# Mask and maximum in one VectorE instruction, a full-height last down block, and three roots by ScalarE

## The chip, the cores and the metric

The kernel runs on one core of a Trainium2 chip. The metric is the device time of one execution in microseconds (us): 378.05 us is the median of three executions of the kernel before. The core has a matrix engine (TensorE, PE in the profile, its weight loads PEld), an elementwise engine (VectorE, DVE), an activation engine (ScalarE, ACT), a general engine (GpSimd, POOL) and a queue that issues transfers (SyncE, SP). Each works through its own list of instructions in order; they wait for each other by counting semaphores.

## The reference

Two transformer layers on `x` of 4 sequences by 256 rows by 256 columns, that is 1024 tokens:

```
x = x + xattn0(layernorm(x), ctx)      # 16 heads, rope, softmax over 256 keys
x = x + ffn0(layernorm(x))             # fp8 emulation: x8 = (x/s).astype(e4m3), s = max|x|/448
                                       # out = (square(relu(x8 @ Wfc8.T * s*sw)) to fp8) @ Wpr8.T
n = layernorm(x)
s = ((ctx @ Wq.T + bq) @ (ctx @ Wk.T + bk).T) / 8 * n      # scores times the normed x
x = x + softmax(where(mask, -inf, s))
n = layernorm(x)
routed = sigmoid(n @ w_router + b) > 0.5
h  = n + rmsnorm(n) * w1 @ wv @ wo     # plus biases
y  = h + (silu(h2 @ w_gate) * (h2 @ w_up)) @ w_down        # h2 = rmsnorm(h) * w2, 704 hidden
x  = x + where(routed, y, n)
```

## The kernel before

The 1024 tokens are eight tiles of 128 rows (`NT = 8`). All inputs of one stage stay on the chip. Each engine has one block of Python that writes its list in the order in which it runs; nothing is planned by a scheduler, so the order of the lines is the order of the work, and a wait stops everything behind it on that engine. `in_order` on VectorE and GpSimd makes an engine wait for its own last instruction.

The stages, with their times in the trace: the 16-head attention fills about the first 253 us. `project_last` leaves four pairs of tiles in the accumulator banks, and `x1_tiles` on VectorE adds each pair to `xs`, takes statistics, and the largest and smallest value of each row. The last pair is written out below it. Its variances go to GpSimd, whose `power(3, ...)` forms the reciprocal root; `newton(3, rstd)` refines it on VectorE, and the largest normed value goes through TensorE (`turn_largest`, `largest_everywhere`) to all rows, as the fp8 scale. TensorE's products for the query and key rows (line 1805) stand ahead of `turn_largest` and wait until the last pair has been added.

Then come the fp8 rows, `expand`, the squares on ScalarE (`z_square`), and from about 280 us `contract(t)`, which needs the two fp8 parts of tile t: `h8_shared` from VectorE, and `h8_halved` from VectorE followed by `rounded_top` on ScalarE. `x2_tile(t)` adds the result to `xs`.

The second attention works in two halves of four tiles: `gate_scores`, `mask_scores`, `largest` on VectorE, `root` on GpSimd, `softmax` (exponentials) on ScalarE, `x3_sums` and `x3_statistics` on VectorE. From these variances the function `newton(n, ...)` makes three reciprocal roots per half (numbers 5, 6, 7 and 9, 10, 11), each from a first value that GpSimd computes by a power. `normalise` and `norm_rows` write the normed rows, `turn_norm(c)` transposes them on TensorE, `turned_copy` on ScalarE copies them, and `attend(c)` multiplies them with the folded value and output weights into one bank per tile. `h_tile` takes the result; the sum of its squares (`h_square_sum`, ScalarE), `h_square`, the third root and `h2_tiles` lead to the next transposes, `turn(2, atbuf, ...)`. On TensorE, `keep_busy` issues products whose result nobody reads.

The gated network works on 512 tokens at a time, in six blocks of the 704 hidden columns: five of 128 and one of 64. `gate_high` and `gate_low` fill two banks, `silus` reads one, `gated` the other; `high_part` and `low_part` split the product into two parts for precision. `down(t, fts)` adds up the blocks of one tile. In a full block a `product` is three products; in the last block the high and the low part lie above each other in one tile of 128 rows (`gated_hi[0:64]` and `gated_hi[64:128]`), so two are enough, and the second used only the upper 64 rows. `wd`, and with it `wd_rest`, holds the last 64 rows of `w_down` twice, above each other.

ScalarE's functions stand in tables that are loaded by an instruction of its own (`ACT_TABLE_LOAD`); the kernel before has two of them, one at the start and one ahead of the first `Silu`.

Of the kernel before, what the change touches and what calls it, by code (L numbers as in the profile page):

```python
# [23 lines left out]
P = 128  # L24
# [14 lines left out]
FP8_SHARED = 240.0  # L39
MASKED = -1.5e35  # L40
# [66 lines left out]
def build(nc, x, ctx_t, ctx_n, blob, const_a, const_b, wq1_t, wk1_t, attn_mask, key_mask,  # L107
          w_fc_t, w_proj_t, small, wv_t, wo, w_gate, w_up, w_down, out):
    with ExitStack() as ctx:
# [3 lines left out]
        def sem(name):  # L113
            return ctx.enter_context(nc.semaphore(name))
# [36 lines left out]
        c_p = sb("c_p", [P, NT])  # L151
        score = sb("score", [P, NT])
# [113 lines left out]
        variance_ready, power_ready = sem("variance_ready"), sem("power_ready")  # L266
        ident16_ready = sem("ident16_ready")
# [173 lines left out]
        def _(pool):  # L441
# [91 lines left out]
            power(3, c_ve[:], minus_half[:], c_y[:])  # L533
# [36 lines left out]
            powers(5, 0, c_ve, c_y)  # L570
            powers(6, 0, c_q, c_y1)
            shifted_tiles(0)
            powers(7, 0, c_ve, c_y)
# [14 lines left out]
        def _(act):  # L588
# [145 lines left out]


# [27 lines left out]
            act.wait_ge(d_small, 16)  # L763
            for i in range(2):
# [38 lines left out]

            act.wait_ge(w8_ready, W8_PIECES)
# [16 lines left out]
            softmax(0)  # L821
            rounded_top(5)

# [28 lines left out]
            for t in range(4):  # L852
                h_square_sum(t)
            rounded_top(7)
            for t in range(4):
                router_score(t)
            tail_copy(0)
            softmax(1)
# [54 lines left out]
        def _(dve):  # L913
# [7 lines left out]
            def newton(n, o, lo=0, hi=NT, of=(c_ve, c_y)):  # L921

                ve, y, w = of[0][:, lo:hi], of[1][:, lo:hi], c_t[:, lo:hi]
                dve.wait_ge(power_ready, n - (n > 4) - (n > 8))
# [105 lines left out]

            def x1_tiles(i):
# [3 lines left out]
                dve.tensor_tensor(xs[:, t:t + 2, :].rearrange("p t d -> p (t d)"), bank[OUT_BANK[i]][:],  # L1035
                                  xs[:, t:t + 2, :].rearrange("p t d -> p (t d)"), ALU.add).then_inc(x1_ready, 1)
# [3 lines left out]
                dve.tensor_reduce(spread[:, 0, t:t + 2], xs[:, t:t + 2, :], AX, ALU.max)  # L1040
# [100 lines left out]
            for t in range(NT - 2):  # L1141
                dve.bn_aggr(mv[:, t, :], stats[:, t, :])
            dve.wait_ge(attn_ready, B)
            dve.tensor_tensor(xs[:, NT - 2:NT, :].rearrange("p t d -> p (t d)"), bank[OUT_BANK[B - 1]][:],
                              xs[:, NT - 2:NT, :].rearrange("p t d -> p (t d)"), ALU.add).then_inc(x1_ready, 1)
# [8 lines left out]
            dve.tensor_reduce(spread[:, 0, NT - 2:NT], xs[:, NT - 2:NT, :], AX, ALU.max)  # L1154
# [4 lines left out]
            dve.tensor_scalar(negmean[:], mean, -1.0, None, ALU.mult)  # L1159
            dve.tensor_tensor(spread[:, 0, :], spread[:, 0, :], mean, ALU.subtract)  # L1160
            in_order(dve.tensor_tensor(spread[:, 1, :], mean, spread[:, 1, :], ALU.subtract))
# [297 lines left out]
        def _(pe):  # L1459
# [505 lines left out]
            for t in (2, 3):  # L1965
                down(t, range(FT1)).then_inc(down_ready, 1)
# [89 lines left out]
```

## Time and profile before

| | |
|---|---|
| median of three executions | 378.05 us (377.94 to 378.34) |
| profiled execution | 376.65 us |
| its span, first to last instruction | 374.5 us |
| busy, share of the span: PE, DVE, ACT, POOL | 96%, 77%, 56%, 47% |
| chain that ended last, by engine | PE 69%, DVE 12%, POOL 9%, ACT 5%, issue 3%, DMA 2% |
| granted TensorE clock, mean | 1.000 |

All times in rows are microseconds from the first instruction of the profiled execution. A row of a timeline gives start, duration, engine, line of the kernel, operation, what is written from what, shapes (partitions x elements) and how many instructions are merged into it; in brackets stands how long the engine stood idle before it and what ended that. Consecutive instructions of one engine overlap a little at their ends. Matmul durations include the time in the pipe, so the distance of two starts is what one costs TensorE. A 32-bit product is often two instructions.

### The profile page before, as it was taken

To read this page: it belongs to the slowest core of one execution; us is meant where nothing else is said; L and a number is where in the kernel's file an instruction comes from. 1 tells how busy PE (TensorE), PEld (TensorE's weight loads), DVE (VectorE), ACT (ScalarE), POOL (GpSimd) and SP (SyncE) were. 2 spreads that over 40 slices of the span, in tenths; PEclk is the share of its full clock that TensorE was granted. 3 is DMA by queue.
4 is the path that set the end of the run, shared out by engine and by line. 5 is a ranking of instruction groups with operands and counts; after the bars stand their busy time and mean duration, and the time that the engine had idled before them with its cause. 6 is when DMAs were issued, how large, how long until landed. Compare 5 with 4: busy or idle time off the path is not lost.

```text
span 374.5 us, 6304 instructions
## 1 busy us (share of the span) xinstructions
PE 360.3 (96%) x2179; PEld 267.8 (72%) x2179; DVE 288.1 (77%) x650; ACT 208.0 (56%) x561; POOL 177.9 (47%) x173
## 2 busy tenths in 40 slices
PE   8899999999999999999999999997999999989996
PEld 8765786777677767767776687873648557778885
DVE  4798698698669786986886667478899989896473
ACT  1514575466647655764666396625976343682240
POOL 2453774486467547754864540492630254146000
PEclk9999999999999999999999999999999999999999
DMA  7639200300301202000004000300000000000101
GB/s 235 235 115 339 83 1 2 112 3 1 115 0 16 98 2 94 22 0 2 0 1 156 2 1 0 110 0 1 2 1 2 0 2 0 1 2 0 44 15 58
DMA packets 9023, 17.48 MB, mean 47 GB/s; under 512 B 2144, under 2 KB 6880, under 8 KB 8096
## 3 DMA queue, kind: packets, MB, share of 16 engines
q1 hardware_dynamic: 8992, 17.08, 13.3%
q8 instruction: 18, 0.29, 0.3%
q14 instruction: 13, 0.11, 0.1%
HBM read 16.03 MB, written 1.05 MB: 46 GB/s over the span
## 4 chain that ended last, share of the span: by engine, by line
PE 69%; DVE 12%; POOL 9%; ACT 5%; issue 3%; DMA 2%; SPq 0%; DVEq 0%; POOLq 0%
PE bank L1552 15%; PE bank L1593 8%; PE bank L1611 7%; PE bank L1602 6%; PE bank L1636 4%; PE bank L1577 4%; POOL prob L471 4%; PE bank L1562 3%; PE bank L1505 3%; PE bank L1856 2%; DVE relu L1197 2%; PE bank L1874 2%; DMA blobs<-in_blob 2%; POOL rot_low L466 2%; PE bank L1472 2%
## 5 line engine op out<-in xcount | busy, mean ns | idle before, releaser
L471 POOL TENSOR_TENSOR prob<-prob,rinv 128x512 f32<-128x512 f32 x64 | 66.0, 1042 | 78.3 <-DVE rinv L1061 78.3
L1552 PE MATMUL bank<-xnT,w 128*128 128x512 f32 x288 | 83.0, 425 | 1.7 <-DVE xnT L958 1.7
L643 ACT ACTIVATE prob<-bank,negmax 128x256 f32<-128x256 f32 x128 | 59.7, 488 | 29.5 <-DVE negmax L1055 29.5
L1055 DVE TENSOR_REDUCE negmax<-bank 128x2 f32<-128x512 f32 x64 | 40.9, 681 | 37.6 <-PE bank L1593 37.6
L1552 PEld LDWEIGHTS bank<-xnT,w 128*128 128x128 f32 x288 | 52.4, 188 | 21.9 <-issue 13.3
L653 ACT COPY probT<-bank 128x512 f32<-128x512 f32 x64 | 35.1, 591 | 23.6 <-PE bank L1602 23.6
L989 DVE TENSOR_TENSOR rot_up<-bank,cb 64x512 f32<-64x512 f32 x64 | 44.1, 689 | 1.6
L466 POOL TENSOR_TENSOR rot_low<-rot_low,rot_up 128x512 f32<-128x512 f32 x32 | 41.0, 1282 | 3.8 <-DVE rot_up L989 3.8
L1602 PE MATMUL bank<-ca,prob 128*128 128x128 f32 x256 | 34.2, 273 | 0.4 <-POOL prob L471 0.4
L1602 PEld LDWEIGHTS bank<-ca,prob 128*128 128x128 f32 x256 | 30.1, 140 | 5.3 <-POOL prob L471 0.8
L1593 PEld LDWEIGHTS bank<-ktmp,uT 64*128 64x128 f32 x256 | 23.4, 186 | 13.4 <-issue 11.3
L1593 PE MATMUL bank<-ktmp,uT 64*128 64x256 f32 x256 | 32.0, 389 | 0.0
L1611 PE MATMUL bank<-probT,kva 128*64 128x256 f32 x256 | 30.7, 382 | 0.0
L1636 PE MATMUL bank<-wkvo,cT 128*128 128x256 f32 x128 | 29.7, 381 | 0.0
L464 POOL TENSOR_TENSOR rot_z<-rot_z 128x512 f32<-128x512 f32 x16 | 20.6, 1290 | 16.4 <-DVE rot_z L989 16.4
L643 ACT ACTIVATION_READ_ACCUMULATOR prob<-bank,negmax 128x1 f32 x128 | 27.9, 218 | 0.0
L1636 PEld LDWEIGHTS bank<-wkvo,cT 128*128 128x128 f32 x128 | 23.5, 190 | 3.9 <-issue 1.2
L1611 PEld LDWEIGHTS bank<-probT,kva 128*64 128x64 f32 x256 | 17.6, 137 | 10.8 <-issue 2.4
L451 POOL TENSOR_TENSOR c_y<-c_ve,minus_half 128x4 f32<-128x4 f32 (+1 forms) x7 | 8.0, 1140 | 33.0 <-DVE c_ve L939 22.2
L984 DVE TENSOR_TENSOR rot_low<-bank,cb 128x512 f32<-128x512 f32 x32 | 22.0, 688 | 1.7 <-PE bank L1552 1.2
L658 ACT COPY cT<-bank 128x512 f32<-128x512 f32 x15 | 8.8, 586 | 25.7 <-PE bank L1611 25.7
L989 DVE TENSOR_TENSOR rot_z<-bank,cb 64x512 f32<-64x512 f32 x32 | 22.0, 689 | 0.4
(225 smaller groups left out, 698.7 us busy)
## 6 DMA issues: line engine op xcount, KB each, us to landing
blobs<-in_blob SPq DMA_DIRECT2D x7, 1024.0 KB, 4.9
xs<-in_x SPq DMA_DIRECT2D x2, 512.0 KB, 4.1
xn<-in_w_fc_t SPq DMA_DIRECT2D x1, 1024.0 KB, 4.8
ctxT<-in_w_proj_t SPq DMA_DIRECT2D x1, 1024.0 KB, 5.3
out<-qk SPq DMA_DIRECT2D x8, 128.0 KB, 1.7
cb<-in_const_b SPq DMA_DIRECT2D x1, 768.0 KB, 8.4
blobs<-in_w_gate SPq DMA_DIRECT2D x1, 704.0 KB, 5.3
blobs<-in_w_up SPq DMA_DIRECT2D x1, 704.0 KB, 6.7
```

The costliest lines, as they stand in the source:

```text
L466: pool.tensor_tensor(low[:, r, :], low[:, r, :], up[:, r, :], ALU.add).then_inc(joined, 1)
L471: pool.tensor_tensor(p[:], p[:], rinv[:, n % PROBS, :].unsqueeze(2).to_broadcast([P, 2, S]), ALU.mult).then_inc(normed, 1)
L643: ins = act.activation(prob[n % PROBS][:, st, :], pS[n % UNITS][:, st * S:(st + 1) * S], ACT.Exp, bias=negmax[:, n % UNITS, st:st + 1], ac ...
L653: act.copy(probT[n % UNITS][:].rearrange("p a s -> p (a s)"), pS[n % UNITS][:]).then_inc(probsT_copied, 1)
L984: dve.tensor_tensor(tokens(rope_parts(m)[0]), tokens(src[:]), angles(cosq, r), ALU.mult)
L989: ins = dve.tensor_tensor(tokens(crossed[to:to + DC, :]), tokens(src[lo:lo + DC, :]), angles(sinq, r, lo, lo + DC), ALU.mult)
L1055: dve.tensor_reduce(negmax[:, n % UNITS, :], pS[n % UNITS][:].rearrange("p (a s) -> p a s", a=2), AX, ALU.max, negate=True).then_inc(max_r ...
L1552: ins = pe.matmul(q_bank(m)[:], w[a][:, k, r * P:(r + 1) * P], x[b][:, k, c * CH:(c + 1) * CH], start=(i == 0), stop=(i == 5))
L1593: ins = pe.matmul(pS[2 * a + h][:, st * S:(st + 1) * S], uT[g % 2][lo:hi, at:at + P], ktmp[lo:hi, b * S:(b + 1) * S], start=True, stop=True)
L1602: ins = pe.transpose(pS[n % UNITS][:, lt * S + st * P:lt * S + (st + 1) * P], prob[n % PROBS][:, st, lt * P:(lt + 1) * P], ident)
L1611: ins = pe.matmul(o[h * DC:(h + 1) * DC, :], kva[:, 2 * b + lt, :], probT[2 * a + h][:, lt, :], start=(lt == 0), stop=(lt == 1))
L1636: return pe.matmul(bank[OUT_BANK[t // 2]][:, t % 2 * D:(t % 2 + 1) * D], cT[:, f, t * P:(t + 1) * P], wkvo[:, f, :], start=(f == 0 and t % ...
```

## The change

- `x1_sum` replaces the sum over a pair of tiles and the reduction for the largest value by one `tensor_tensor_reduce` per tile, which writes the sum and its maximum; `mask_scores` does the same for the mask and the maximum over a row of scores, and `largest` only forms the product.
- The reciprocal roots 3, 5 and 7 come from ScalarE's `Sqrt` and VectorE's `reciprocal` instead of GpSimd's power, still with a Newton step. `load_table` issues an activation of one column whose result nobody reads, so that the table is loaded there: for `Sqrt` behind the last context copies, for `Exp` ahead of `rounded_top(0)`, for `Sqrt` behind `softmax(0)`, for `Exp` ahead of `softmax(1)`.
- VectorE's steps for the first scale are interleaved with the Newton step; `h8_halved(6)` and `x2_tile(6)` move further down VectorE's list.
- `attend` works on pairs of tiles and waits for each half of the columns by itself. Two blocks of `down(0)` come ahead of `attend(1)`, with the wait for the fifth gated product; `down(2)` comes ahead of `turn(2, ..., (2, 3))`.
- The last block of `down` uses all 128 rows in its second product as well.

```diff
+LEAST = -3.0e38
+ROOTED = (3, 5, 7)
+POWERED = (1, 2, 6, 9, 10, 11)
 # GpSimd
-            power(3, c_ve[:], minus_half[:], c_y[:])
...
-            powers(5, 0, c_ve, c_y)
             powers(6, 0, c_q, c_y1)
             shifted_tiles(0)
-            powers(7, 0, c_ve, c_y)
 # ScalarE
+            def load_table(function):
+                act.activation(unread[:], ones[:, 0:1], function)
+            def square_roots(n, lo, hi):
+                act.wait_ge(variance_ready, n)
+                act.activation(c_y[:, lo:hi], c_ve[:, lo:hi], ACT.Sqrt).then_inc(sqrt_ready, 1)
+            act.wait_ge(ones_ready, 1)
+            load_table(ACT.Sqrt)
...
             act.wait_ge(d_small, 16)
+            square_roots(3, 0, NT)
...
+            load_table(ACT.Exp)
             act.wait_ge(w8_ready, W8_PIECES)
             rounded_top(0)
...
             softmax(0)
+            load_table(ACT.Sqrt)
             rounded_top(5)
+            square_roots(5, 0, NT // 2)
...
             for t in range(4):
                 h_square_sum(t)
+            square_roots(7, 0, NT // 2)
             rounded_top(7)
             for t in range(4):
                 router_score(t)
             tail_copy(0)
+            load_table(ACT.Exp)
             softmax(1)
 # VectorE
             def newton(n, o, lo=0, hi=NT, of=(c_ve, c_y)):
-                dve.wait_ge(power_ready, n - (n > 4) - (n > 8))
+                if n in ROOTED:
+                    dve.wait_ge(sqrt_ready, ROOTED.index(n) + 1)
+                    in_order(dve.reciprocal(y, y))
+                else:
+                    dve.wait_ge(power_ready, POWERED.index(n) + 1)
...
+            def x1_sum(i):
+                for a in range(2):
+                    t = 2 * i + a
+                    ins = dve.tensor_tensor_reduce(out=xs[:, t, :], in0=bank[OUT_BANK[i]][:, a * D:(a + 1) * D],
+                                                   in1=xs[:, t, :], scale=1.0, scalar=LEAST, op0=ALU.add, op1=ALU.max,
+                                                   accum_out=spread[:, 0, t:t + 1])
+                return ins
             def x1_tiles(i):
-                dve.tensor_tensor(xs[:, t:t + 2, :].rearrange("p t d -> p (t d)"), bank[OUT_BANK[i]][:],
-                                  xs[:, t:t + 2, :].rearrange("p t d -> p (t d)"), ALU.add).then_inc(x1_ready, 1)
+                x1_sum(i).then_inc(x1_ready, 1)
...
-                dve.tensor_reduce(spread[:, 0, t:t + 2], xs[:, t:t + 2, :], AX, ALU.max)
...
-            dve.tensor_reduce(spread[:, 0, NT - 2:NT], xs[:, NT - 2:NT, :], AX, ALU.max)
             in_order(dve.tensor_reduce(spread[:, 1, NT - 2:NT], xs[:, NT - 2:NT, :], AX, ALU.min))
             dve.wait_ge(variance_ready, 3)
-            dve.tensor_scalar(negmean[:], mean, -1.0, None, ALU.mult)
-            dve.tensor_tensor(spread[:, 0, :], spread[:, 0, :], mean, ALU.subtract)
+            dve.wait_ge(sqrt_ready, 1)
+            dve.reciprocal(c_y[:], c_y[:])
+            in_order(dve.tensor_scalar(negmean[:], mean, -1.0, None, ALU.mult))
+            dve.scalar_tensor_tensor(out=c_t[:], in0=c_y[:], scalar=-0.5, in1=c_y[:], op0=ALU.mult, op1=ALU.mult)
+            in_order(dve.tensor_tensor(spread[:, 0, :], spread[:, 0, :], mean, ALU.subtract))
+            dve.tensor_tensor(c_t[:], c_t[:], c_ve[:], ALU.mult)
             in_order(dve.tensor_tensor(spread[:, 1, :], mean, spread[:, 1, :], ALU.subtract))
+            dve.scalar_tensor_tensor(out=rstd[:], in0=c_t[:], scalar=1.5, in1=c_y[:], op0=ALU.add, op1=ALU.mult)
             in_order(dve.tensor_tensor(spread[:, 2, :], spread[:, 0, :], spread[:, 1, :], ALU.max))
-            newton(3, rstd)
...
             def mask_scores(gr):
-                in_order(dve.tensor_tensor(xn[:, lo:hi, :], xn[:, lo:hi, :], mbias[:, lo:hi, :], ALU.add))
+                for t in range(lo, hi):
+                    ins = dve.tensor_tensor_reduce(out=xn[:, t, :], in0=xn[:, t, :], in1=mbias[:, t, :], scale=1.0,
+                                                   scalar=LEAST, op0=ALU.add, op1=ALU.max, accum_out=c_m[:, t:t + 1])
+                in_order(ins)
             def largest(gr):
-                in_order(dve.tensor_reduce(c_m[:, lo:hi], xn[:, lo:hi, :], AX, ALU.max, negate=True))
                 dve.wait_ge(root_ready, gr + 1)
-                dve.tensor_tensor(c_b[:, lo:hi], c_m[:, lo:hi], rstd[:, lo:hi], ALU.mult).then_inc(gated_ready, 1)
+                dve.scalar_tensor_tensor(out=c_b[:, lo:hi], in0=c_m[:, lo:hi], scalar=-1.0, in1=rstd[:, lo:hi],
+                                         op0=ALU.mult, op1=ALU.mult).then_inc(gated_ready, 1)
...
             x3_statistics(0)
-            h8_halved(6)
             newton(5, rstd, 0, half)
...
             dve.wait_ge(variance_ready, 6)
+            h8_halved(6)
             newton(6, r1, 0, half, of=(c_q, c_y1))
...
-            x2_tile(6)
             dve.wait_ge(variance_ready, 7)
             newton(7, r2, 0, half)
             h2_tiles(0)
+            x2_tile(6)
 # TensorE
             def attend(c):
-                pe.wait_ge(turned_copied, 6 + 2 * c)
-                for t in range(4 * c, 4 * c + 4):
+                for two in (4 * c, 4 * c + 2):
                     for k in range(DK):
-                        ins = pe.matmul(res_bank(t)[:, 0:DV], tailT[:, k, t * P:(t + 1) * P], wvo[:, k, :],
-                                        start=(k == 0), stop=(k == DK - 1))
-                    ins.then_inc(res_ready, 1)
+                        pe.wait_ge(turned_copied, 4 + 2 * c + k + 1)
+                        for t in (two, two + 1):
+                            ins = pe.matmul(res_bank(t)[:, 0:DV], tailT[:, k, t * P:(t + 1) * P], wvo[:, k, :],
+                                            start=(k == 0), stop=(k == DK - 1))
+                            if k == DK - 1:
+                                ins.then_inc(res_ready, 1)
...
-                        ins = pe.matmul(o, gated_hi[0:m, ft, cols], wd_rest[0:m, ft, :], start=False, stop=True)
+                        ins = pe.matmul(o, gated_hi[:, ft, cols], wd_rest[:, ft, :], start=False, stop=True)
...
-            def down_two(t):
-                down(t, range(FT1 - 1))
+            def down_two(t, done=0):
+                down(t, range(done, FT1 - 1))
...
             turn_norm(1)
-            pe.wait_ge(act_ready, 4)
+            pe.wait_ge(act_ready, 5)
+            down(0, range(2))
             attend(1)
-            pe.wait_ge(act_ready, 5)
-            down_two(0)
+            down_two(0, 2)
+            pe.wait_ge(h_ready, 6)
+            pe.wait_ge(score_ready, 6)
+            down(2, range(FT1)).then_inc(down_ready, 1)
             pe.wait_ge(score_ready, NT)
             turn(2, atbuf, h2_ready, 0, (2, 3))
-            for t in (2, 3):
-                down(t, range(FT1)).then_inc(down_ready, 1)
+            down(3, range(FT1)).then_inc(down_ready, 1)
```

## Rows read from the trace of the kernel before

**Rows 1.** Two stretches: length, busy PE, PEld, DVE, ACT, POOL, clock, DMA share, GB/s.
```profile
10.00:20.00 10.00, 8.13 (x50) 6.60 (x48) 7.30 (x18) 5.59 (x13) 5.59 (x8) 1.00 0.60 199
...
314.00:330.00 16.00, 15.62 (x68) 12.45 (x69) 13.89 (x42) 9.40 (x21) 5.85 (x9) 1.00 0.00 1
```

**Rows 2.** Timeline from 253 to 258.4 us: VectorE, GpSimd, TensorE.
```profile
253.19 0.69 DVE L1144 TENSOR_TENSOR xs<-bank,xs 128x512 f32<-128x512 f32 x1 [0.25 <-PE bank L1636]
...
255.66 0.67 DVE L1155 TENSOR_REDUCE spread<-xs 128x2 f32<-128x512 f32 x1
...
255.23 1.67 POOL L451 TENSOR_TENSOR c_y<-c_ve,minus_half 128x8 f32<-128x8 f32 x1 [1.46 <-DVE c_ve L1153]
...
253.93 3.64 PE L1805 MATMUL bank<-ctx,wqk 64*64 64x512 f32 x8 [0.78 <-DVE xs L1144]
258.11 0.30 PE L1764 MATMUL bank<-ca,pad 128*128 128x128 f32 x1 [0.54 <-DVE pad L1165]
```

**Rows 3.** Timeline of VectorE from 289 to 294 us: gate product, mask, maximum.
```profile
289.46 1.70 DVE L1236 SCALAR_TENSOR_TENSOR xn<-xs,mv,qk 128x256 f32<-128x256 f32 x4
291.20 1.22 DVE L1242 TENSOR_TENSOR xn<-xn,mbias 128x1024 f32<-128x1024 f32 x1
292.46 1.22 DVE L1246 TENSOR_REDUCE c_m<-xn 128x4 f32<-128x1024 f32 x1
```

**Rows 4.** Timeline of ScalarE from 296 to 324 us.
```profile
296.27 1.04 ACT L801 ACTIVATE tail_all<-prob 128x1024 bf16<-128x1024 fp8e4 x1
...
310.65 0.70 ACT L849 ACTIVATE score<-bank,sm 128x1 f32<-128x1 f32 x4
...
321.52 1.28 ACT L865 ACT_TABLE_LOAD   x1
322.82 1.09 ACT L865 ACTIVATE tail_all<-bank 128x512 f32<-128x512 f32 x2
```

**Rows 5.** Timeline from 294 to 309 us: TensorE, and GpSimd's power.
```profile
294.68 3.73 PE L1856 MATMUL bank<-wpr,tail_all 128*128 128x256 bf16 x32
298.25 3.83 PE L1760 MATMUL bank<-wfc,ident 128*128 128x512 bf16 x17
302.78 1.48 PE L1865 MATMUL bank<-ca,xn 128*128 128x128 f32 x8 [0.71 <-DVE xn L943]
...
304.99 3.74 PE L1874 MATMUL bank<-cb,tailT 128*128 128x257 f32 x16
...
300.29 1.23 POOL L451 TENSOR_TENSOR c_y<-c_ve,minus_half 128x4 f32<-128x4 f32 x1 [7.53 <-DVE c_ve L939]
```

**Rows 6.** Waits, whole span: total us, times, longest us.
```profile
ACT xn L816 <- DVE c_b L1248: 7.8, 2, 4.3
...
ACT proj L768 <- PE bank L1805: 7.2, 2, 7.0
...
ACT tail_all L801 <- DVE bf_m L1297: 3.6, 4, 2.1
...
PE bank L1552 <- DVE xnT L958: 1.7, 1, 1.7
```

**Rows 7.** Timeline from 331 to 336 us: ScalarE, TensorE, VectorE.
```profile
331.78 0.61 ACT L865 ACTIVATE tail_all<-bank 128x512 f32<-128x512 f32 x1
...
332.04 3.71 PE L1874 MATMUL bank<-cb,tailT 128*128 128x257 f32 x16 [0.82 <-ACT tailT L593]
...
332.86 0.68 DVE L1370 TENSOR_TENSOR tail_all<-bank,tail_all 128x512 f32<-128x512 f32 x1
```

**Rows 8.** Timeline of TensorE from 343.4 to 344.4 us: last block of `down(2)`.
```profile
343.40 0.28 PE L1474 MATMUL bank<-wd_high,gated_lo 128*128 128x256 f32 x1
343.52 0.28 PE L1933 MATMUL bank<-wd_high,gated_hi 128*128 128x256 f32 x1
343.73 0.38 PE L1934 MATMUL bank<-wd_rest,gated_hi 64*128 64x256 f32 x1
344.04 0.38 PE L1472 MATMUL bank<-wd_high,gated_hi 128*128 128x256 f32 x1
```

More of the change, by code:

```diff
@@ L151, in build @@
         c_p = sb("c_p", [P, NT])
+        unread = sb("unread", [P, 1])
         score = sb("score", [P, NT])
@@ L266, in build @@
         variance_ready, power_ready = sem("variance_ready"), sem("power_ready")
+        sqrt_ready = sem("sqrt_ready")
         ident16_ready = sem("ident16_ready")
@@ L1143, in _ @@
             dve.wait_ge(attn_ready, B)
-            dve.tensor_tensor(xs[:, NT - 2:NT, :].rearrange("p t d -> p (t d)"), bank[OUT_BANK[B - 1]][:],
-                              xs[:, NT - 2:NT, :].rearrange("p t d -> p (t d)"), ALU.add).then_inc(x1_ready, 1)
+            x1_sum(B - 1).then_inc(x1_ready, 1)
             dve.wait_ge(x1_ready, B)
```

## The prediction

> **What bounds the kernel now.** I read the page's busy shares and its slices first, then the table by stretches, the list of waits and the timelines of the stages that the diff touches. TensorE is busy nearly everywhere; in the gate stage, for instance, 15.62 of 16 us [rows 1]. It is not the only limit: in the serial passages between the products VectorE, ScalarE or GpSimd set the pace, and the reader should see TensorE standing for each: before the transposed maximum, before the norm transposes, before the second `attend` [rows 2, 5, 7]. So an edit pays in two ways: by shortening such a passage, or by taking time from TensorE's own stream at the end. An edit on VectorE beneath a full TensorE pays nothing.
>
> **Part 1, end of the first attention.** Only the last pair of tiles is on the path. Before: one sum of 0.69 us at 253.19; TensorE's eight products for the query and key rows start behind it at 253.93; GpSimd's power takes 1.67 us from 255.23; the second reduction ends at 256.33; the transpose that waits for the maximum starts at 258.11 [rows 2]. Now two fused instructions of 256 columns replace the sum and the maximum. The trace has no such instruction. The nearest row with two tensors and a scalar is the gate product, 1.70 for four, 0.425 each [rows 3]; the low bound is a quarter of the 1024-column add, 0.31; the high bound is an add and a reduction one after the other, 0.61 [rows 3]. I take 0.425, and 0.48 for the last, whose end is not overlapped: 0.91 for 0.69, so what follows starts 0.22 later. One reduction (0.67 [rows 2]) goes. The root is now a ScalarE instruction of some 0.25 us (four 1-column instructions took 0.70 [rows 4]; low bound 0.17, high bound 0.5, half a 1024-column one [rows 4]) in place of 1.67 us, and it ends beneath the remaining reduction. VectorE then adds a reciprocal and interleaves the Newton steps with the spreads. Four interleaved steps at 0.27 and two single ones at 0.2, from 256.0 on, put the maximum at about 257.45. TensorE is the next limit: its products start 0.22 later and occupy it 3.5 us (8 in 3.64, the last still in the pipe [rows 2]), until 257.65. The transpose therefore moves from 258.11 to about 257.66: **-0.45** (-0.65 at the low price of the fused instruction, -0.1 at the high one). The square root stands ahead of the four `proj1` copies on ScalarE's queue and delays them some 0.3 us; who reads them comes four us later. The other three pairs of tiles wait for TensorE anyway, so their edit is costed at nothing; without that cover each pair would cost 0.2 and save 0.67. The table for the root is loaded inside ScalarE's wait of 7.0 us, the return to the exponential's inside one of 2.1 us, the last return inside one of 4.3 us [rows 6]: nothing, if a load is 1.28 us as in rows 4 and its one-column companion 0.25.
>
> **Part 2, first half of the second attention.** Masking and maximum took 2.48 us (291.20 to 293.68 [rows 3]); four fused at 0.425 take 1.70, so the exponentials start and end 0.78 earlier, at 295.5. But behind them on ScalarE now stands a table load: 1.30 from its start to the next activation, and 0.25 for the unread one [rows 4]. So the rounding of tile 5's upper halves, which began at 296.27, begins at 297.05 and ends at 298.1. TensorE needs it for the last 8 of the 32 products that start at 294.68 (0.11 each [rows 5]); they would begin at 297.4 and now begin at 298.1. The 17 filler products then start 0.75 later, at 299.0, and last 3.7 (3.83 with the last one's tail [rows 5]), to 302.7. VectorE's side gains more: 0.78 from the mask, and GpSimd's power (1.23 from 300.29 [rows 5]) gives way to a ScalarE root and a reciprocal, some 0.6 less. The first normalised rows are there at 301.3 instead of 302.6, and nobody takes them. TensorE's wait of 0.71 [rows 5] goes, and in its place stands the filler: transposes at 302.7 instead of 302.78. They gain a little inside, since all four tiles are ready (1.48 before, I take 1.1), so `attend(0)` starts at 304.65 instead of 304.99. Its new order by pairs delivers each pair's first tile later and the last tile as before. Of these 0.35 some 0.2 is given back: the rounding of tile 7, which ended near 310.65 [rows 4], stands behind the root of the third variance, which waits for VectorE. **-0.15** at the gate stage (-0.45 at the low price, +0.6 at the high one). `x2_tile(6)` behind `h2_tiles(0)` and `h8_halved(6)` behind the norm move work that nobody awaits at that moment; uncovered they would cost their 0.75 to 0.9 once. The same fusion in the second half lies beneath the gate stage's full TensorE [rows 1]: nothing now.
>
> One rule of the Trainium skill speaks against this part: ScalarE: Activation LUTs, What ACT_TABLE_LOAD costs, adds a drain of about 1.38 us to each switch. Our load ends at 322.80 and the next activation starts at 322.82 [rows 4], so the trace shows none. What a drain would do here is the third rival.
>
> **Part 3, second attend and first down products.** The new order puts two blocks of `down(0)` ahead of `attend(1)` and makes TensorE wait for the fifth gated product. That one comes from a chain that begins with TensorE's own norm transposes: copies, then `silu` (331.78, 0.61), then the product on VectorE (0.68) [rows 7]. TensorE had finished the transposes at 331.22 (0.82 before 332.04 [rows 7]). If VectorE takes the product right behind `silu`, it ends at 333.1, a wait of about 2.0; at its old place, 333.54, it is 2.4. So 1.2 us more standing (up to 1.6). The transposes themselves gain about 0.25, as their rows come earlier. The wait is then repaid by part 4; the square sums, the power and the second norm run beneath `down_two(0, 2)` and `down(2)`, so the later `attend(1)` costs nothing more.
>
> **Part 4, the last block of each down product.** Within `down(2)` the 128-row products follow each other at 0.12 (343.40 to 343.52). The 64-row one does not: 0.21 passes from the one ahead of it, 0.31 until the next, and that next one itself lasts 0.10 longer [rows 8]. A block pair costs 0.52 and would cost 0.24; with what follows it the saving is 0.28 to 0.38, I take 0.335. Four such blocks stand in the first half: -1.34, with +1.2 and -0.25 of part 3 **-0.4**. Four stand at the very end, with nothing but TensorE ahead of the last output: **-1.34**.
>
> By a rule of the Trainium skill (TensorE: Matmul & The Clock Gate, Why this matters for your kernels) a product with few rows takes the same time as a full one; our rows differ in the neighbour's start, 0.31 against 0.12 [rows 8]. What that would leave of the sum is the fourth rival.
>
> **Sum.** -0.45 - 0.15 - 0.4 - 1.34 = -2.34. The profiled execution took 376.65 (span 374.5, 2.15 around it), so 374.3. The median of the runs shown, 378.05, lies 1.40 above it; with the same distance, **375.7**. Low prices of the fused instruction give 375.2, a wait of 2.4 in part 3 gives 376.1; with small errors in each term its own range is 375.0 to 376.4.
>
> **The rivals.** First: the fused instruction takes as long as the two that it replaces, 0.61. For it: it does the work of both, and no row shows one. Against: the gate product, with as many operands, takes 0.425 [rows 3]. Part 1 falls to -0.1, and the exponentials start 0.75 later than I say, which reaches TensorE through the rounding, +0.6: the sum is -1.25, 376.8.
> Second, the other side: TensorE's clock drops in the new wait of 2 us. The granted clock is 1.00 in the stretches of rows 1, also in the one that holds TensorE's longest wait so far, 1.7 us [rows 1, 6]; the new one is longer. At the lower of the two levels (1.2 GHz) the six products and `attend(1)` behind it, 0.8 and 3.4, would double: +4.2 and the sum +1.9, 379.9. It decides once more than 2.3 us of products run at that level.
> Third: ScalarE must run empty ahead of a load, and a switch costs twice the load's 1.28. That adds 1.3 behind the first exponentials, which TensorE's rounding wait passes on; the return in the wait of 2.1 us [rows 6] no longer fits by 0.75, of which the first contraction hides some 0.5. So +1.55, the sum -0.8, 377.25. For it: four new loads behind busy stretches. Against: the two starts of rows 4, 1.30 apart.
> Fourth, the change doesn't do what it says: 128 rows cost what 64 did. Parts 3 and 4 lose 2.7: +0.35, 378.4. The spacing in rows 8 is all against it.
>
> **How the numbers follow.** The forecast 0.70; slow fusion 0.10; clock 0.07; drain 0.07; no gain by rows 0.06. From 374.8 to 377.4 lie nearly all of the forecast, slow fusion and the drain. Measurement can tell about 0.2%, 0.76 us, so faster means under 377.3: nearly all of the first case, most of slow fusion, a part of the drain: 0.80. Within: 0.12. Slower, over 378.8: the clock and a remainder, 0.08.
>
> **What would show it.** Fused instructions of 0.42 to 0.48 and exponentials about 0.8 earlier; a load of 1.28 behind the first exponentials, with TensorE's transposes now right behind the filler; a wait of 2.0 to 2.4 us ahead of `down(0)`, at clock 1.00; 0.12 at each last block; the last product some 2.3 us earlier. The forecast is wrong if the fused instruction is over 0.6, if that wait exceeds 3 us, or if the last blocks keep their 0.31.

## The result, and the profile after

The changed kernel takes 372.97 us (median of four executions, 372.17 to 376.51; the kernel before 378.0 beside it, 377.94 to 378.34): a ratio of 0.990 [0.987, 0.993]. The forecast was 375.7, with 374.8 to 377.4. The direction was right; the gain is 5.0 us where 2.3 were forecast, and the time lies below the range.

Part of these 5.0 is no work at all. TensorE's granted clock falls in some executions of either kernel. By its granted clock an execution of the kernel before falls into one of two groups: 59 at a mean of 0.998 or more take 376.59 (375.92 to 377.46), 27 below that take 378.12 (377.57 to 378.82). The changed kernel takes 372.84 in 8 (372.16 to 373.51) and 374.86 in 10. The four executions of the kernel before that stand beside the result, around 378.0, have the times of its second group; their clock is not on record, so that they fell is inferred from their times. Three of the four of the changed kernel had a clock of 1.000. At full clock the change is worth **3.7 us**. Two of the twelve executions of one variant below (`no_fuse`) took 1033 and 1042 us; they stay out of its ratio and of all counts.

The ledger goes by TensorE's starts, in one trace of each kernel at full clock (the two are `before_again` and `after_third` below). The traces of each kernel agree in these distances to 0.04 us wherever the clock stays up:

| from - to | forecast | before | after | difference |
|---|---|---|---|---|
| query and key products (254) - transposed maximum | -0.45 | 4.17 | 3.57 | -0.60 |
| - first gate product (313) | -0.15 | 56.21 | 55.13 | -1.08 |
| - second half's norm transposes (328) | 0 | 15.51 | 15.17 | -0.34 |
| - first product of the network's second half (344) | -0.40 | 16.58 | 15.80 | -0.78 |
| - end of the last product | -1.34 | 25.00 | 23.56 | -1.44 |
| sum | -2.34 | 117.47 | 113.23 | -4.24 |

The products of the first line start at 253.6 in the one and at 254.6 in the other; 0.09 of that is the change (a wait of 0.87 for 0.78). The rest is there by the tenth microsecond (TensorE's second group of products starts at 8.99 and at 9.98), ahead of all that the change touches, and varies from execution to execution of the same work (253.55 to 254.65 in the traces of the changed kernel and its variants), which is why the executions as a whole give less than 4.24.

The end of the first attention, timeline of the changed kernel at full clock (answers to [rows 2]):

```profile
253.76 0.42 DVE L1058 CUSTOM_DVE_ANT_0 xs<-bank,xs 128x256 f32<-128x256 f32 x1 [0.76 <-PE bank L1671]
...
254.11 0.42 DVE L1058 CUSTOM_DVE_ANT_0 xs<-bank,xs 128x256 f32<-128x256 f32 x1
254.46 0.08 DVE L1058 DVE_READ_ACCUMULATOR2_ANT spread<- 128x1 f32 x1
...
254.60 3.65 PE L1840 MATMUL bank<-ctx,wqk 64*64 64x512 f32 x8 [0.87 <-DVE spread L1058]
...
255.91 0.21 ACT L744 ACTIVATE c_y<-c_ve 128x8 f32<-128x8 f32 x1 [5.45 <-DVE c_ve L1182]
...
257.75 0.16 DVE L1197 TENSOR_REDUCE pad<-spread 128x1 f32<-128x8 f32 x1
...
258.17 0.33 PE L1799 MATMUL bank<-ca,pad 128*128 128x128 f32 x1
```

The fused instruction is named `CUSTOM_DVE_ANT_0`. One lasts 0.42, but the next starts 0.35 after it, and the read of the maximum (0.08) lies beneath its neighbour. The transpose has no wait any more: it follows TensorE's products.

The second attention, the same trace (answers to [rows 3 to 5]):

```profile
291.20 0.42 DVE L1275 CUSTOM_DVE_ANT_0 xn<-xn,mbias 128x256 f32<-128x256 f32 x1
...
292.25 0.42 DVE L1275 CUSTOM_DVE_ANT_0 xn<-xn,mbias 128x256 f32<-128x256 f32 x1
...
295.17 0.18 ACT L831 ACTIVATION_READ_ACCUMULATOR xn<-xn,c_b,rstd 128x1 f32 x1
295.37 1.28 ACT L739 ACT_TABLE_LOAD   x1
...
296.67 0.20 ACT L739 ACTIVATE unread<-ones 128x1 f32<-128x1 f32 x1
296.77 1.04 ACT L815 ACTIVATE tail_all<-prob 128x1024 bf16<-128x1024 fp8e4 x1
297.87 1.05 PE L1891 MATMUL bank<-wpr,tail_all 128*128 128x256 bf16 x8 [0.65 <-ACT tail_all L815]
298.97 3.62 PE L1795 MATMUL bank<-wfc,ident 128*128 128x512 bf16 x16
...
302.42 1.04 PE L1900 MATMUL bank<-ca,xn 128*128 128x128 f32 x8
```

Four fused instructions take 1.47 (291.20 to 292.67), where mask and maximum took 2.48. The load stands where the prediction saw it, TensorE waits 0.65 for the rounding behind it, and the transposes follow the filler at once.

The execution profiled with the result (376.51) is one in which the clock fell. Its stretches of 2 us, columns as in [rows 1], and the first products behind the new wait:

```profile
253.00:255.00 2.00, 1.28 (x3) 0.45 (x4) 1.90 (x10) 0.00 (x0) 0.47 (x1) 1.00 0.00 0
255.00:257.00 2.00, 2.00 (x5) 0.69 (x4) 1.79 (x11) 1.37 (x4) 0.00 (x0) 0.74 0.00 0
257.00:259.00 2.00, 2.00 (x4) 0.42 (x3) 0.04 (x1) 0.97 (x2) 0.00 (x0) 0.50 0.00 0
...
261.00:263.00 2.00, 2.00 (x6) 1.61 (x7) 1.81 (x8) 1.40 (x4) 0.00 (x0) 0.56 0.00 0
...
332.00:334.00 2.00, 0.85 (x7) 0.85 (x8) 1.69 (x3) 1.86 (x4) 0.00 (x0) 1.00 0.01 4
334.00:336.00 2.00, 2.00 (x8) 1.64 (x7) 0.00 (x0) 0.00 (x0) 0.00 (x0) 0.61 0.04 8
336.00:338.00 2.00, 2.00 (x6) 1.56 (x5) 1.63 (x4) 0.51 (x2) 0.00 (x0) 0.53 0.00 0
338.00:340.00 2.00, 2.00 (x14) 1.83 (x14) 1.71 (x5) 1.90 (x8) 0.00 (x0) 1.00 0.00 0
```

```profile
333.15 0.39 PE L1507 MATMUL bank<-wd_high,gated_hi 128*128 128x256 f32 x1 [2.17 <-DVE tail_all L1405]
```

0.50 is the lower of the two levels (1.2 GHz for 2.4). It came twice: behind the wait for the last pair of tiles, within the 64-row products, from 255.9 to 262.8, and behind the new wait of 2.17 ahead of `down(0)`, from 334.4 to 337.9. Beside the trace at full clock the first cost 2.35 us (61.05 for 58.70 from the query and key products to the first gate product) and the second 1.67 (17.47 for 15.80 in the ledger's fourth line).

### The profile page after: what moved, and what is told of

Read it like the earlier page. It is cut to its first block, busy times and chain, and to the rows that moved or that the text cites. A ratio compares the mean times of both kernels' runs of the same rounds, so it can differ in the third digit from the quotient of the medians.

```text
span 374.0 us, 6334 instructions
## 1 busy us (share of the span) xinstructions
PE 361.0 (97%) x2179; PEld 270.6 (72%) x2179; DVE 285.7 (76%) x673; ACT 214.3 (57%) x572; POOL 172.7 (46%) x170
## 2 busy tenths in 40 slices
DMA packets 9023, 17.47 MB, mean 47 GB/s; under 512 B 2145, under 2 KB 6881, under 8 KB 8097
## 4 chain that ended last, share of the span: by engine, by line
PE 77%; DVE 12%; POOL 5%; ACT 4%; issue 1%; DVEq 0%; POOLq 0%
PE bank L1587 15%; PE bank L1628 8%; PE bank L1646 8%; PE bank L1671 8%; PE bank L1637 6%; PE bank L1612 4%; PE bank L1597 3%; PE bank L1540 3%; POOL prob L476 2%; PE bank L1910 2%; PE bank L1697 2%; DVE relu L1229 2%; PE bank L1891 2%; POOL rot_low L471 2%; PE bank L1547 1%; PE bank L1507 1%
## 5 line engine op out<-in xcount | busy, mean ns | idle before, releaser
L1795 PE MATMUL bank<-wfc,ident 128*128 128x512 bf16 (+1 forms) x74 | 17.8, 359 | 0.0
```

## The experiments

Each stood beside executions of the kernel before on the same chip; ratios are against that. "Full clock" means executions with a mean granted clock of 0.998 or more. A time at full clock, often the median of few executions, still holds the 1.1 us by which the start varies; where it differs from the distances within a trace, the distances are the ones to go by.

**The two kernels again.** `after_again`, later `after_third`: the changed kernel as it is. `before_again`: the kernel before as it is.

> The changed kernel once more, for a trace in which TensorE's clock holds. Theory A: the two stretches at 1.2 GHz in the first trace (from 255.9 and from 334.3 us) cost about 1.9 and 1.7 us of its 374.0 us span and come in some executions only; where the granted clock is 1.00 the span is near 370.4 and the time near 372.5. Theory B: the drop belongs to the new waits and comes in most executions; then the median stays near 375 and the spans near 374.

> The kernel before, unchanged, for its granted clock in several executions. Its profiled execution took 376.65 at clock 1.00, the others 377.94 to 378.34. Theory A: the others lost about 1.4 us at the lower level of the clock in the stage from 253 us, so that a clock of about 0.995 stands beside 378.0 and 1.00 beside 376.6, and the true difference of the two kernels at full clock is about 4.1 us. Theory B: their clock is 1.00 as well, the difference of 1.4 us lies outside the span or is scatter, and the change is worth 5 us.

> The changed kernel as it is, as the measure for the three beside it. 372.8 us in executions at a mean granted clock of 1.000; each fall of the clock (mean 0.995) adds about 2 us, and by the kernels with the same wait ahead of down(0) it comes in half of the executions or more.

Measured: 373.41, ratio 0.991 [0.989, 0.994]; 377.01, 1.000 [0.999, 1.002]; 374.1, 0.992 [0.989, 0.995]. The changed kernel's clock fell in 11 of the 22 executions listed so far; the two groups lie 2.0 us apart.

**Only the 128-row last block** (`rows128`), put into the kernel before:

```diff
-ins = pe.matmul(o, gated_hi[0:m, ft, cols], wd_rest[0:m, ft, :], ...)
+ins = pe.matmul(o, gated_hi[:, ft, cols], wd_rest[:, ft, :], ...)
```

> The kernel before with part 4 alone: the last down block uses 128 rows in its second product. By the spacing (0.52 to 0.24 us for the pair, 0.34 for each block) the end gains 1.34. The first four blocks gain 1.34 on TensorE, but the first two of them end in a wait for the second norm's rows, so only down(2) and down(3), about 0.7, count: -2.0 in all, 376.0. Rival (a product with few rows takes the same time as a full one): 378.0.

Measured: 375.96, ratio 0.998 [0.996, 1.000]. The trace is plainer than the ratio: at full clock the span is 372.0 us for 374.4, but outside its span an execution of this variant spent 3.2 us at the median where one of the kernel before spent 2.15, for a reason that the record does not show. From the second half's first product to the end it shows 23.57 for 25.00, so -1.43; in the first half only -0.62 of the same four blocks. The last blocks, and what takes the rest:

```profile
339.06 0.28 PE L1933 MATMUL bank<-wd_high,gated_hi 128*128 128x256 f32 x1
339.18 0.28 PE L1934 MATMUL bank<-wd_rest,gated_hi 128*128 128x256 f32 x1
340.07 1.47 PE L1467 MATMUL bank<-ca,at_rows 128*128 128x128 f32 x8 [0.62 <-DVE at_rows L1289]
```

The spacing is 0.12, as said. But TensorE now arrives 0.62 early at the second norm's transposes and waits for VectorE: part 4 alone loses half of its first term there, which `down(2)` ahead of the transposes wins back.

**TensorE's old order** (`old_order`), in the changed kernel (lines joined and shortened here):

```diff
-pe.wait_ge(act_ready, 5); down(0, range(2)); attend(1); down_two(0, 2); down(2, ...)
+pe.wait_ge(act_ready, 4); attend(1); pe.wait_ge(act_ready, 5); down_two(0)
 turn(2, atbuf, h2_ready, 0, (2, 3))
-down(3, ...)
+down(2, ...); down(3, ...)
```

> The changed kernel with TensorE's old order at the second attend: attend(1) first, then the wait for the fifth gated product, down_two(0), the transposes, down(2) and down(3). If the new order pays by giving TensorE two blocks ahead of attend and down(2) in place of the wait for the second norm, undoing it costs 0.3 to 0.8 us (373.3 to 373.8). If the new wait of 2.2 us ahead of down(0) costs more than that (my forecast for part 3 without part 4: +0.9), undoing it gains up to 0.9 (372.1) and TensorE's longest wait there is 0.8 us or less.

Measured: 371.82, ratio 0.988 [0.985, 0.990]; at full clock 371.80 against 372.84. The new order of part 3 is a loss, of 0.4 by the distances (15.43 for 15.80) and of 1.0 by the times. What the old order pays is seen at the second norm's transposes, 0.93 ahead of them and, as the rows come one tile after another, 0.4 inside them (1.46 for the 1.04 of eight without a wait):

```profile
338.07 1.46 PE L1502 MATMUL bank<-ca,at_rows 128*128 128x128 f32 x8 [0.93 <-DVE at_rows L1324]
```

**The good half of each order** (`attend_first`): from the kernel just told, `down(2)` goes back ahead of those transposes. **And the load behind the rounding** (`attend_first_late_load`):

```diff
 softmax(0)
-load_table(ACT.Sqrt)
 rounded_top(5)
+load_table(ACT.Sqrt)
 square_roots(5, 0, NT // 2)
```

> The changed kernel with attend(1) ahead of all of down(0), as before the change, and down(2) ahead of the second norm's transposes, as changed. Theory: TensorE's wait of 2.2 us ahead of down(0) was a loss, and the other half of the reorder is a gain, since down(2) covers the 0.93 us in which TensorE otherwise waits for the scaled rows: 0.9 under the kernel with the whole old order (371.8), so about 370.9, and 1.9 under the changed one. Rival: the second network's first products then wait for the copies of the transposes (1.27 on ScalarE, 1.40 on VectorE behind 1.42 of sums), only 1.9 of down(3) lies between, and the 0.9 comes back: about 371.8.

> As the run before, and the load of the root's table behind the rounding of tile 5 instead of ahead of it. Theory: TensorE's wait of 0.65 us for that rounding goes and the filler products start that much earlier; the normed rows, ready about when the filler then ends, take 0.1 to 0.2 of it back: -0.5 against the run before, about 370.4. Rival: the norm's rows set the start of the transposes anyway, the 0.65 turns into a wait for them: same as the run before.

Measured: 371.1, ratio 0.985 [0.982, 0.987], and 370.21, 0.982 [0.980, 0.985]. At full clock 370.80 and 370.20: both forecasts held. The stretch of the ledger's fourth line takes 13.93 where the changed kernel takes 15.80 and the old order 15.43. With the later load:

```profile
293.88 3.66 PE L1891 MATMUL bank<-wpr,tail_all 128*128 128x256 bf16 x32
...
295.76 1.28 ACT L739 ACT_TABLE_LOAD   x1
...
301.04 1.04 PE L1900 MATMUL bank<-ca,xn 128*128 128x128 f32 x8
```

All 32 products run without a wait, and from the first to the transposes pass 7.16 instead of 7.98.

**Without the fused instructions** (`no_fuse`): sum and mask by `tensor_tensor`, both maxima by `tensor_reduce`, as before the change. **Without them in the second half alone** (`gate_unfused`).

> The changed kernel without its fused instructions: sum, mask and both maxima stand as in the kernel before, all else as changed. Theory now: the fused instruction is cheaper than I priced it (four in 1.48 us where mask and maximum took 2.48 and where I had 1.70), and VectorE's time around it is on TensorE's path in three places: 0.3 to 0.5 us at the end of the first attention, about 1.0 ahead of the second half's rounding and norm, and 0.3 to 0.4 in the gate stage, where the low parts that TensorE waits for stand behind the mask on VectorE's queue. So +1.6 to +2.0 us over the changed kernel's 372.8. Rival, the prediction's own account: 0.2 to 0.4 at the end of the attention, 0.15 at most in the second half, nothing in the gate stage: +0.4 to +0.6.

> The changed kernel with mask and maximum of the second half as two instructions again (1.22 each against 1.48 for the four fused). Theory: in the gate stage VectorE is late as well, since the low parts of the first half, for which TensorE waits, stand behind the mask on its queue: 1.0 us later there, of which TensorE loses 0.4 to 0.5, and the wait ahead of down(0) grows by up to 0.5: +0.4 to +1.0 at full clock. Rival, the prediction's account: it lies beneath the gate stage's full TensorE: 0.

Measured: 376.48, ratio 0.999 [0.996, 1.001], and 375.28, 0.995 [0.992, 0.997]. At full clock 374.48 (one execution) and 373.33. By distances `no_fuse` loses 0.49 at the end of the attention, 0.26 and 0.76 ahead of the first norm transposes, and 0.45 in the gate stage (behind that the clock fell in its trace). From the transposed maximum to the first gate product it takes 56.22, as the kernel before does (56.21): the whole gain of the ledger's second line hangs on the fusion. `gate_unfused` loses the same 0.45 there and 0.51 behind it, 1.0 in all. VectorE's low parts and the products that read them, with two instructions:

```profile
316.08 1.22 DVE L1276 TENSOR_REDUCE c_m<-xn 128x4 f32<-128x1024 f32 x1
...
317.41 1.40 DVE L1392 SCALAR_TENSOR_TENSOR tail_lo<-bank,sm,tail_hi 128x512 fp32r<-128x512 f32 x2
318.29 0.41 PE L1963 MATMUL bank<-tail_lo,wgu_high 128*128 128x512 f32 x1
318.87 2.79 PE L1963 MATMUL bank<-tail_lo,wgu_high 128*128 128x512 f32 x11 [0.16 <-DVE tail_lo L1392]
```

and fused:

```profile
317.02 1.40 DVE L1388 SCALAR_TENSOR_TENSOR tail_lo<-bank,sm,tail_hi 128x512 fp32r<-128x512 f32 x2
318.94 2.88 PE L1959 MATMUL bank<-tail_lo,wgu_high 128*128 128x512 f32 x12
```

Counted from the first gate product, the low parts start at 4.73 without the fusion (317.41 from 312.68) and at 3.72 with it (317.02 from 313.30); in the one case TensorE stands for them, in the other they are there. The kernel before has the same delay, with no idle time of over 0.03 in it:

```profile
319.98 3.22 PE L1922 MATMUL bank<-tail_lo,wgu_high 128*128 128x512 f32 x12
```

3.22 against 2.88 for the same twelve products: 0.34, the ledger's third line.

**Without the roots and loads** (`no_roots`): GpSimd's power for 3, 5 and 7, no table loaded ahead.

> The changed kernel with the reciprocal roots 3, 5 and 7 by GpSimd's power again and no table loaded ahead. Theory: the first root costs about 0.4 us at the maximum (a power of 1.67 in place of 0.2 and a reciprocal of 0.18, of which most lies beside the reduction); the second costs VectorE 0.6, but without the load TensorE's wait of 0.65 for the rounding of tile 5 goes too, so 0 to 0.3 net; the third is hidden beneath the seventh and eighth contraction. Sum +0.4 to +0.7. Rival A: the roots are the larger part of what the prediction missed, three powers of 1.67, 1.23 and 1.2 against three roots of 0.4: +1.5 or more. Rival B: the loads eat the roots up: 0 or below.

Measured: 375.66, ratio 0.996 [0.994, 0.998]; at full clock 373.54 (two executions), +0.7, as said; by the distances 1.3. But the terms differ from both accounts:

```profile
254.85 1.67 POOL L456 TENSOR_TENSOR c_y<-c_ve,minus_half 128x8 f32<-128x8 f32 x1 [1.55 <-DVE c_ve L1177]
256.65 0.17 DVE L1183 TENSOR_SCALAR negmean<-mv 128x8 f32<-128x8 f32 x1 [1.29 <-POOL c_y L456]
...
258.20 0.30 PE L1793 MATMUL bank<-ca,pad 128*128 128x128 f32 x1 [1.00 <-DVE pad L1191]
...
294.45 3.66 PE L1885 MATMUL bank<-wpr,tail_all 128*128 128x256 bf16 x32
...
301.61 1.44 PE L1894 MATMUL bank<-ca,xn 128*128 128x128 f32 x8
```

The first root is worth 1.07: the reduction that used to cover the power is gone, and what now stands behind the root on VectorE's list waits with it. The fifth, with its load in front of the rounding, is a loss: without it the transposes come 0.82 earlier and cost 0.39 more, net 0.43. The loss is the load's place: with the load behind the rounding the root gains 0.4 (8.91 from the fifth contraction to `attend(0)`, for 9.30 with the power). Around the seventh, 0.2 is gained, and 0.5 behind the second half's transposes (1.36 for 1.04, and a wait of 2.38 ahead of `down(0)`).

**The clock.** `filled_wait`: nine products that nobody reads in the wait ahead of `down(0)`. `long_wait`: the same wait made longer.

```diff
 turn_norm(1)
+keep_busy(9, 3)                 # filled_wait
 pe.wait_ge(act_ready, 5)
+pe.wait_ge(gated_low, 4)        # long_wait
```

> The changed kernel with nine products of 512 columns, whose result nobody reads, in TensorE's wait of 2.2 us ahead of down(0) (9 by 0.22 is 2.0, so they end inside it). Theory: the wait itself lets the granted clock fall to its lower level, which costs about 2 us in the executions where it comes; filled, the time at full clock stays at 372.8, at most 0.1 more, and falls are as rare as in the kernel before (8 of 23 executions) or rarer, so the median comes to about 372.8 and at least 1 us under that of the changed kernel in this job. Rival: the clock falls at other places (ahead of the 64-row products at 254 us), or by chance from outside: then as many executions with a fall as beside it.

> The changed kernel with TensorE's wait ahead of down(0) made longer: it also waits for the fourth low part, which VectorE finishes about 0.6 us behind the fifth product, so 2.8 us instead of 2.2. Theory: the longer TensorE stands there, the more often its granted clock falls behind the wait: 0.4 of the executions or so at 2.2 us, about 0.75 with the three kernels that wait 2.4; at 2.8 nearly all, each for about 2 us, so about 373.4 in the few at full clock and a median of 375.4. Rival: the falls are chance: about as many as without a long wait, 1 in 4, and a median of 373.4.

Measured: 372.42, ratio 0.988 [0.985, 0.992], and 375.69, 0.997 [0.995, 0.999]. The wait in each, and the stretches of the longer one:

```profile
329.60 1.89 PE L1795 MATMUL bank<-wfc,ident 128*128 128x512 bf16 x8
331.71 0.39 PE L1507 MATMUL bank<-wd_high,gated_hi 128*128 128x256 f32 x1 [0.23 <-DVE tail_all L1405]
```

```profile
332.00:334.00 2.00, 0.00 (x0) 0.00 (x0) 1.95 (x3) 1.95 (x4) 0.21 (x1) 1.00 0.01 4
334.00:336.00 2.00, 1.95 (x9) 1.79 (x10) 0.00 (x0) 0.16 (x1) 0.00 (x0) 0.71 0.03 8
336.00:338.00 2.00, 2.00 (x6) 1.54 (x6) 0.37 (x1) 0.00 (x0) 0.00 (x0) 0.50 0.00 0
```

Executions below a mean clock of 0.998, by what TensorE waits for ahead of `down(0)`:

| kernels | wait, us | below / all | of these at 0.994, 0.995 or 0.986 | full clock; below |
|---|---|---|---|---|
| `old_order`, `attend_first` and the two late loads | none of over 0.4 | 5 / 23 | 2 | 371.80, 370.80, 370.20, 369.78; some 2 more |
| `filled_wait` | filled, 0.23 left | 2 / 6 | 0 | 371.86; 374.15 |
| the changed kernel | 2.2 | 11 / 22 | 6 | 372.84; 374.86 |
| `no_fuse`, `no_roots`, `gate_unfused` | 2.4 | 28 / 34 | 25 | 374.48, 373.54, 373.33; 376.35, 375.76, 375.40 |
| `long_wait` | 2.8 | 11 / 12 | 8 | 373.99; 375.82 |

The third column mixes two falls, and the mean clock can tell them apart. In the three traces that hold a fall, the one behind this wait lasts 3.4 us and the one at 256 us lasts 6.8: `no_fuse`, with the first alone, has a mean of 0.995; the result's trace and `long_wait`, with both, have 0.986. The second alone would give 0.991 (an estimate: 6.8 us at half the clock in a span of 371). So the fourth column counts the falls that can lie behind this wait. They are rare where it is filled or absent, 6 of 22 at 2.2 us, 25 of 34 at 2.4 and 8 of 12 at 2.8; the others do not grow with it (3 of 23, 2 of 6, 5 of 22, 3 of 34, 3 of 12). That a longer wait lets the clock fall more often is borne out up to 2.4 us; the place of each single fall is not shown, since the kernel before, without this wait, has 19 of 86 executions at 0.994 or 0.995. Six executions of `filled_wait` are few.

**Filling the wait at 254 us** (`best_filled`): `attend_first_late_load` and four products that nobody reads ahead of the 64-row products.

> The fastest kernel so far (attend(1) first, late load) with four products of 512 columns, whose result nobody reads, in TensorE's wait of 0.87 us ahead of the 64-row products at 254 us. Theory: same time at full clock, 370.2 (at most 0.1 more), and the falls of the clock in the long stage behind that wait, which the kernel before has too, go: no execution below 0.998. Rival: the 64-row products, not the wait ahead of them, let the clock fall, or the falls have nothing to do with this place: as many as before (1 in 5, 2 in 6).

Measured: 369.91, ratio 0.981 [0.978, 0.984], the fastest kernel of this study; full clock 369.78. One execution of six still fell to 0.994, so this filler does not settle whether that wait or the 64-row products let the clock fall.

**Where the kernel before loses its clock** (`before_look1` to `before_look3`), three profiled executions.

> The kernel before, one profiled execution, to see where its clock falls in the third of its executions in which it does. Theory: 378.0 (the median that the forecast started from) is an execution with such a fall, behind the wait for the last pair of tiles at 253 us and its 64-row products (mean clock 0.991) or behind the wait ahead of the second attend (0.995); at full clock 376.4. Rival: 378.0 comes from elsewhere in the span, at full clock.

Measured: 376.26, 376.35 and 376.23, all at 0.999. None caught a fall, so its place in that kernel stays open.

## Why the prediction was wrong, point by point

Three steps failed: the level that the sum was added to, the size of part 2, and the fusion in the second half, which was put at nothing. Part 3 came out better than forecast because of effects that the forecast does not hold.

**The level.** The distance of 1.40 between the profiled execution (376.65, clock 1.000) and the median was added to the forecast as if it belonged to both kernels. It is about what a fall costs in the kernel before (378.12 against 376.59). That the executions beside the result fell was not recorded; it is inferred from their times. At the same clock as its starting point the forecast is 374.3, against 372.84: 1.4 of the miss of 2.7 is this step, and the rest lies in the terms.

**Part 1, right.** -0.45 forecast, -0.51 measured (-0.60 and the 0.09 at the start). The fused price was 0.425 and 0.48 for the last; it is 0.35 to the next, and TensorE's products are the next limit, as said.

**Part 2, the step that failed by size.** -0.15 forecast, -1.08 measured. Four fused took 1.47, not 1.70. The load's cost to TensorE was right (0.7 said, 0.65 of waiting, 0.82 between starts in the experiment). What was mis-sized came ahead of it and behind it: a gain of 0.24 ahead of the fifth contraction, because `h8_shared(4)`, for which it waits, stands behind the mask on VectorE's queue, was missing (`no_fuse` loses it again); `attend(0)` gained 0.57 counted from there, not 0.35; and the 0.2 given back by the rounding of tile 7 became a gain of 0.22. The fusion carries the first two (`no_fuse` loses 0.26 and 0.76 there) and the roots the last (`no_roots` loses 0.2 there), but with their loads the roots cost 0.24 over the whole stretch (54.89 without them). The moves of `h8_halved(6)` and `x2_tile(6)` were not tried alone; what part of the last two gains is theirs is open.

**"Beneath the gate stage's full TensorE: nothing", wrong.** The row cited for it, 15.62 busy of 16 [rows 1], could not show it. Of its 0.38 of idle time 0.35 is the wait for the first gate product (314.00 to 314.35) and 0.03 lies at the low parts; the rest of their delay counts as busy, because a product's duration includes its time in the pipe and covers a late start of the next. The distances show it: 3.22 for 2.88 over twelve products. By the distances the fusion in the second half is worth 1.0 on the path (0.45 there, 0.51 behind it), by the times 0.5 (three executions); 0.34 of it appears as the third line of the ledger.

**Part 3, mechanism right, balance wrong.** The wait is 2.17 (2.0 to 2.4 said) and the transposes take 1.04. "The wait is then repaid by part 4" hid that the reorder is two edits: `down(2)` ahead of the transposes is worth 1.5 (15.43 to 13.93), `down(0)` ahead of `attend(1)` costs 1.9 (15.80 for 13.93). Together they cost 0.37, where the prediction puts part 3 as a whole at +0.95. Without the reorder the stretch already goes from 16.58 to 15.43; the wait ahead of `attend(1)` is 0.33 in `old_order` where the kernel before has 0.82, which the prediction leaves out. Whether the waiting for each half by itself or the earlier rows bring that was not tried.

**Part 4, right at the end** (-1.44 for -1.34), and half hidden in the first half when alone (`rows128`).

**The rivals.** The fused instruction is not slow (0.35 for 0.61). The rows do count (0.12 for 0.31); whether their number costs it or the change between neighbours of different height was not separated. The load at 295.37 starts 0.02 behind the end of ScalarE's instruction ahead of it, and the activation behind it 1.30 after its start (296.67): no drain on either side. The drain of 1.38 of the Trainium skill (ScalarE: Activation LUTs, What ACT_TABLE_LOAD costs) is thus not seen at these loads either. The clock does fall behind the new wait, as the second rival said, by the mean clock in 6 of 22 executions; there it costs 1.67, not 4.2, since the lower level lasted from 334.4 to 337.9 and not over all the products behind the wait.

## What to carry to other kernels

Before adding up terms, look at which clock the starting time was taken, and add them to a profile at that clock alone. A TensorE that is 98% busy can still be waiting: a late start of 0.1 to 0.2 us hides in the duration of the product ahead of it. Compare the distances of starts with those of equal products elsewhere before an edit on another engine is costed at nothing. Cost a reorder edit by edit, each move by itself; here one half was worth 1.5 us and the other cost 1.9.

## What the runs showed of the hardware that was not expected

- A VectorE instruction with two inputs and a maximum over 256 columns lasts 0.42 and follows the one before it after 0.35: less than two passes (0.61) and than the gate product (0.425).
- TensorE's granted clock fell to the lower level for 3.4 us behind waits of 2.2, 2.4 and 2.8 us ahead of `down(0)` (the result's trace, `no_fuse`, `long_wait`); in the result's trace this cost 1.67 us. By the mean clock such falls came in 6 of 22, 25 of 34 and 8 of 12 executions.
- The other place where it fell lies behind a wait of only 0.87, within products of 64 rows and 64 columns (255.9 to 262.8 us); it cost 2.35 us. Whether the wait or these products let it fall stays open.
